# Attention with a running maximum: the pieces that find each row's maximum are computed for two heads at once, on half the rows of TensorE's array each

## The reference

```python
q = (x @ Wq).reshape(b, n, HEADS, DIM_HEAD).transpose(0, 2, 1, 3)
k = (context @ Wk).reshape(b, m, HEADS, DIM_HEAD).transpose(0, 2, 1, 3)
v = (context @ Wv).reshape(b, m, HEADS, DIM_HEAD).transpose(0, 2, 1, 3)
scores = jnp.einsum('bhnd,bhmd->bhnm', q, k) * scale
attn = jax.nn.softmax(scores, axis=-1)
out = jnp.einsum('bhnm,bhmd->bhnd', attn, v)
out = out.transpose(0, 2, 1, 3).reshape(b, n, HIDDEN)
return out @ Wo + bo
```

## Time and profile before

| | us |
|---|---|
| median of 3 runs | 1034.98 (1029.81 to 1036.09) |
| profiled execution | 1032.15 |
| its span, first to last instruction | 1030.3 |
| mean granted TensorE clock | 0.967 of full speed |
| busy: PE / weight loads / DVE / ACT / POOL | 947.4 / 556.1 / 586.7 / 360.5 / 563.2 |

### The profile page before, as it was taken

How to read it: one execution, slowest core, us unless ns; L and a number is a source line. 1 busy time by engine, 2 the same in 40 slices (tenths; PEclk the granted TensorE clock), 3 DMA queues, 4 the chain that set the end, 5 groups by cost and what they waited for, 6 DMA issues and landing times. The chain is left out here.

```text
span 1030.3 us, 12668 instructions
## 1 busy us (share of the span) xinstructions
PE 947.4 (92%) x3784; PEld 556.1 (54%) x3785; DVE 586.7 (57%) x1212; ACT 360.5 (35%) x506; POOL 563.2 (55%) x346
## 2 busy tenths in 40 slices
PE   6978699999999999999999999999899999999940
PEld 3544355555565555565555555545578888666620
DVE  5997566666667667657668658653744122144424
ACT  2254244434434434425443425443441111122202
POOL 4452187797767787767779768774005200022224
PEclk9998899999999999999999999999899999999975
DMA  8214600100001100001100001030593100322215
GB/s 272 57 41 122 168 11 11 32 0 11 11 1 52 31 1 11 11 0 51 31 11 0 11 8 45 11 106 38 171 342 141 41 1 0 122 78 84 75 36 168
DMA packets 45730, 62.19 MB, mean 60 GB/s; under 512 B 3600, under 2 KB 35216, under 8 KB 45680
## 3 DMA queue, kind: packets, MB, share of 16 engines
q1 hardware_dynamic: 40160, 53.85, 17.7%
q0 software_dynamic: 2256, 6.17, 1.7%
q10 hardware_dynamic: 3264, 1.57, 0.5%
HBM read 36.45 MB, written 17.59 MB: 52 GB/s over the span
## 5 line engine op out<-in xcount | busy, mean ns | idle before, releaser
L641 POOL TENSOR_TENSOR accG<-accG,probs 128x1024 f32<-128x1024 f32 (+1 forms) x170 | 404.1, 2377 | 59.9 <-ACT probs L675 44.9
L728 DVE TENSOR_REDUCE mxp<-mx 128x1 f32<-128x402 f32 x480 | 260.5, 571 | 97.4 <-PE mx L851 81.5
L675 ACT ACTIVATE probs<-st 128x1024 f32<-128x1024 f32 (+1 forms) x208 | 211.4, 1025 | 278.6 <-PE st L874 156.3
L886 PE MATMUL av<-probs,V 128*64 128x512 f32 (+1 forms) x832 | 192.4, 600 | 0.0
L874 PE MATMUL st<-Q,K 65*128 65x512 f32 (+1 forms) x416 | 159.1, 400 | 0.0
L886 PEld LDWEIGHTS av<-probs,V 128*64 128x64 f32 (+1 forms) x832 | 54.1, 136 | 102.4 <-issue 90.2
L851 PE MATMUL mx<-K,Q1b 128*128 128x400 f32 (+1 forms) x256 | 98.2, 384 | 1.2 <-DVE Q1b L716 0.9
L874 PEld LDWEIGHTS st<-Q,K 65*128 65x128 f32 (+1 forms) x416 | 75.7, 185 | 24.0 <-issue 12.4
L851 PE MATMUL mx<-K,Q1a 128*128 128x402 f32 x224 | 85.9, 383 | 0.2
L641 POOL TENSOR_TENSOR accG<-probs 128x1024 f32<-128x1024 f32 x16 | 38.2, 2386 | 79.9 <-ACT probs L675 68.1
L1512 POOL DMA_INDIRECT scratch_routed<-ysb,row x31 | 29.8, 961 | 85.1 <-DMA scratch_routed<-ysb,row 53.9
(11 more groups left out here) (196 smaller groups left out, 1184.4 us busy)
## 6 DMA issues: line engine op xcount, KB each, us to landing
w_gate_up<-in_gate_up SPq DMA_DIRECT2D x4, 2048.0 KB, 19.7
w_down<-in_down SPq DMA_DIRECT2D x2, 2048.0 KB, 14.8
xs<-scratch_sorted_x SPq DMA_DIRECT2D x31, 128.5 KB, 2.1
scratch_sorted_x<-zero SPq DMA_DIRECT2D x7, 514.0 KB, 7.6
K<-K SPq DMA_DIRECT2D x8, 400.5 KB, 4.8
xT<-in_xT SPq DMA_DIRECT2D x4, 512.0 KB, 8.5
xring<-in_x SPq DMA_DIRECT2D x4, 512.0 KB, 8.5
scratch_x1b<-xT SPq DMA_DIRECT2D x4, 512.0 KB, 3.3
```

The costliest lines, as they stand in the source:

```text
L641: pool.tensor_tensor(accG[0:r], so_far[0:r], probs[0:r, (p * KT + t) % RING], ALU.add).then_inc(g_add, 1)
L675: act.activation(probs[0:r, s], st[g % 2][0:r, :], ACT.Exp, scale=DH ** -0.5).then_inc(a_probs, 1)
L728: dve.tensor_reduce(mxp[:, par, u, j:j + 1], mx[(par + n) % 2][:, 0:kn], AX.X, ALU.max).then_inc(v_mx, 1)
L886: mm = pe.matmul(av[h * DH:(h + 1) * DH, :], V[0:r, t, (2 * p + h) * DH:(2 * p + h + 1) * DH], probs[0:r, g % RING, h * QC:(h + 1) * QC], ...
```

## The change

A piece now uses the high part of the queries alone, which is one half of the array's rows. The two heads' pieces for the same queries and keys are issued as a pair: head 0 on rows 0 to 63 into bank 0, head 1 on rows 64 to 127 into bank 1. For this the second head's queries are stored the other way round, low part on partitions 0 to 63 and high part on 64 to 127; the sum over all 128 rows is the same. A step has 16 pairs instead of 32 pieces. The first matmul of a pair waits for both reductions of the pair before, VectorE waits for both matmuls and then reduces twice. Every tile has one pair, behind `scores_2`; tiles 5, 9 and 11 have a second one between `scores_1` and `scores_2`. Nothing stands between the two matmuls of `scores_2` any more. The divisions come after pairs 5 and 10. SyncE copies the high part in two transfers.

```diff
 def query_high(_):
-        act.activation(Q1[0:DH, h], banks[2][DH * h:DH * h + DH, :], ACT.Copy).then_inc(a_q0, 1)
+        act.activation(Q1[DH * h:DH * h + DH, h], banks[2][DH * h:DH * h + DH, :], ACT.Copy).then_inc(a_q0, 1)
...
-PIECES_AT = (1, 1, 3, 3, 3, 3, 3, 3, 2, 3, 3, 2, 2)
-DIVIDE_AFTER = (11, 11, 22, 22)
+TWO_PAIRS_AT = (5, 9, 11)
+PIECE_PAIRS = QT * len(KC)
+DIVIDE_AFTER = (5, 5, 10, 10)
...
-                sp.dma_start(Q2[0:DH, par].bitcast(F32), Q1[par][0:DH].bitcast(F32)).then_inc(d_q2[par], 16)
+                for h in range(2):
+                    sp.dma_start(Q2[0:DH, par, h].bitcast(F32), Q1[par][DH * h:DH * h + DH, h].bitcast(F32)).then_inc(d_q2[par], 16)
...
-                act.activation(Q1[par][0:DH, h], mx[par][DH * h:DH * h + DH, :], ACT.Copy).then_inc(a_hi, 1)
+                act.activation(Q1[par][DH * h:DH * h + DH, h], mx[par][DH * h:DH * h + DH, :], ACT.Copy).then_inc(a_hi, 1)
...
             def piece_maxima(F, par, after_piece):
 
-                for u in range(2 * QT):
+                for i in range(QT):
                     for j, (k0, kn) in enumerate(KC):
-                        n = len(KC) * u + j + 1
-                        dve.wait_ge(p_mx, F * (STEP_MX - 1) + n)
-                        dve.tensor_reduce(mxp[:, par, u, j:j + 1], mx[(par + n) % 2][:, 0:kn], AX.X, ALU.max
-                                          ).then_inc(v_mx, 1)
+                        n = len(KC) * i + j + 1
+                        dve.wait_ge(p_mx, F * (STEP_MX - 1) + 2 * n)
+                        for h in range(2):
+                            dve.tensor_reduce(mxp[:, par, h * QT + i, j:j + 1], mx[h][:, 0:kn], AX.X, ALU.max
+                                              ).then_inc(v_mx, 1)
                         after_piece(n)
...
             def max_scores(F, pair, par, use, n, after=None):
 
-                u, j = (n - 1) // len(KC), (n - 1) % len(KC)
-                h, i = u // QT, u % QT
+                i, j = (n - 1) // len(KC), (n - 1) % len(KC)
...
-                pe.wait_ge(v_mx, use + (n - 1))
-                pe.matmul(mx[(par + n) % 2][:, 0:kn], Q1[par][:, h, i * P:(i + 1) * P], K1[:, 2 * pair + h, k0:k0 + kn],
-                          start=True, stop=True).then_inc(p_mx, 1)
+                pe.wait_ge(v_mx, use + (2 * n - 1))
+                for h in range(2):
+                    rows = slice(DH * h, DH * h + DH)
+                    pe.matmul(mx[h][:, 0:kn], Q1[par][rows, h, i * P:(i + 1) * P], K1[rows, 2 * pair + h, k0:k0 + kn],
+                              start=True, stop=True).then_inc(p_mx, 1)
...
                     for t in range(2, KT):
                         scores_1(c, p, t)
+                        if t in TWO_PAIRS_AT:
+                            next_piece()
+                        scores_2(c, p, t)
                         next_piece()
-                        scores_2(c, p, t, next_piece)
-                        if PIECES_AT[t] > 2:
-                            next_piece()
```

More of the change, by code:

```diff
@@ L354, in query_low @@
                     dve.wait_ge(a_q0, h + 1)
-                    dve.tensor_tensor(Q1[DH:P, h], banks[2][DH * h:DH * h + DH, :], Q1[0:DH, h].bitcast(F32), ALU.subtract
+                    dve.tensor_tensor(Q1[DH - DH * h:P - DH * h, h], banks[2][DH * h:DH * h + DH, :],
+                                      Q1[DH * h:DH * h + DH, h].bitcast(F32), ALU.subtract
                                       ).then_inc(v_q0, 1)
@@ L715, in q_low @@
                     dve.wait_ge(a_hi, F * 2 + (h + 1))
-                    ins = dve.tensor_tensor(Q1[par][DH:P, h], mx[par][DH * h:DH * h + DH, :],
-                                            Q1[par][0:DH, h].bitcast(F32), ALU.subtract).then_inc(v_lo, 1)
+                    dve.tensor_tensor(Q1[par][DH - DH * h:P - DH * h, h], mx[par][DH * h:DH * h + DH, :],
+                                      Q1[par][DH * h:DH * h + DH, h].bitcast(F32), ALU.subtract).then_inc(v_lo, 1)
                 dve.wait_ge(v_lo, F * 2 + 2)
@@ L798, in chunk @@
                     else:
-                        for n in range(1, STEP_MX):
+                        for n in range(1, PIECE_PAIRS + 1):
                             after_piece(n)
@@ L864, in scores_1, with scores_2 @@
                               start=True, stop=False)
-            def scores_2(c, p, t, between=None):
+            def scores_2(c, p, t):
                 g, r = p * KT + t, rows_of(t)
@@ L869, in scores_2 @@
                 if t == 0:
-                    pe.wait_ge(d_q2[par], (c * 2 + (p // 2 + 1)) * 16)
+                    pe.wait_ge(d_q2[par], (c * 2 + (p // 2 + 1)) * 32)
                     pe.wait_ge(d_m[par], (c * 2 + (p // 2 + 1)) * 32)
@@ L875, in scores_2 @@
                                    Q2[0:DH + 1, par, h], start=False, stop=True)
-                    if h == 0 and between is not None:
-                        between()
                 mm.then_inc(p_qk, 1)
@@ L945, in next_piece @@
                         done[0] += 1
-                        if ahead and done[0] < STEP_MX:
+                        if ahead and done[0] <= PIECE_PAIRS:
                             max_scores(F, pair, par, use, done[0], c * QT if p == 1 and not first else None)
```

## The result

The changed kernel takes 1145.1 us, the median of four runs (1127.5 to 1156.0), against 1033.6 for the kernel before (four runs, 1029.8 to 1036.1). The ratio is 1.096, 95% interval 1.086 to 1.106; it is taken without the two longest runs (1156.0 and 1153.5, mean granted clock 0.900), and the two others took 1136.7 and 1127.5 at 0.921 and 0.928. I had forecast slower, 1086 us with a range to 1126: the direction is right, half of the size is missing, and every run lies above the range. The profile shown is of the execution of 1156.0 us, so it shows the clock at its worst.

The account below looks back on a forecast made before the run. The prediction took a two-bank handshake between TensorE and VectorE as the bound, not a busy engine. Stages of 24.02 against 20.61 us give +3.41 a step, +51 over 15 steps: 1083 profiled, 1086 us median, range 1062 to 1126.

Parts of the forecast that it names:

- The handshake: Between successive pairs in the attention stages: a pair waits for both reductions of the one before, at least 1.61 us.
- the same four terms: From pair to pair: matmul to reduction 0.39 us, two reductions 1.06, release of the weight load 0.06, unhidden weight load 0.10.
- Stages 7.47, 7.47, 9.08: Forecast us for a step's three stretches with pairs, A, B and C, against 7.42, 6.84 and 6.35 before.
- the +51 us: Forecast growth over 15 attention steps, from +3.41 us a step in the three stages.
- Side by side: In each pair: its two half-row matmuls run at once, so a pair takes the time of one piece.
- The rival of a serial pair: A pair's two matmuls run one after the other: +6.3 us a step, 1126 to 1129 us; chance 12%.
- Switches: Changing array shape into half rows: 0.19 us into a first pair of each stage; on the way out inside the handshake.
- Cheap handshake: Rival for the stages: weight load hidden and no switch, +1.5 us a step, 1055 to 1058 us; chance 7%.
- PE relieved: Rival: stages bound by PE's columns, so halving helps: 3.6 us less a step, 978 to 981 us; chance 4%.
- the fourth rival: Clock: PE waits more, a third of the stages fall to 1.2 GHz, +66 us on top, about 1150; chance 4%.
- The sign that the prediction itself gave for being wrong: In the stages: a granted clock under 1; also listed were one-pair tiles under 1.5 us or stage C under 7.
- the price of a tile: In stages at 1.2 GHz: 0.92 us of score matmuls becomes 1.84 and the pair adds 0.2, 1.1 us a tile.

Follow-up runs that it names:

- more columns in the waits: Changed kernel with the two scores_1 matmuls of tiles 1, 5, 9 and 11 issued a second time while PE waits for the pair's reductions: 1092.6 us.
- short reductions: Every reduction reads 100 of 400 columns: 1038.8 us on the changed kernel (pairs), 1005.6 us on the kernel before (single pieces on full rows).
- pairs, own waits: Changed kernel, but each matmul of a pair waits only for its own bank and each reduction only for its own matmul: 1077.3 us.
- pairs, own waits and in the values: Changed kernel with separate bank waits for each matmul of a pair, and second pairs moved into the blocks of values: 1067.7 us.
- pairs, three in the values: Changed kernel with the second pairs of tiles 5, 9 and 11 moved into the three blocks of values, divisions after pairs 6 and 11: 1091.4 us.
- pairs on the same half: Changed kernel, but both matmuls of a pair take rows 0 to 63, so they run one after the other: 1261.8 us.

## Where the prediction was right, and where it failed

**The handshake.** Right. "From one pair to the next it takes at least 1.61 us": 1.63 measured, from the same four terms. Stages 7.47, 7.47, 9.08 were 7.55, 7.55, 9.18, and the +51 us were +55. The run with more columns in the waits, which keeps the clock behind the first step, is 63 us above the kernel before beside it (1092.6 against 1029.8): the 55, and some 6 us by which the lower clock lengthens its first step more than that of the kernel before.

**Side by side.** Right: the two records of a pair last 0.45 us together, as long as a single half-row piece (208.76 above), and on full rows, one after the other, the handshake is 0.15 longer. The rival of a serial pair falls.

**Switches.** Right in size: 0.2 us each way, shown by the half-row pieces in the order of before (0.39 for two). The Trainium skill, TensorEngine Tiling (Array Packing), Key Properties, says that a change of tiling mode drains the engine. 65 rows against 64, both matmuls in a row, agree with it here: stage B at full clock is 8.15 us with the one and 8.32 with the other. The weight of the switches was understated: short reductions show that the switches alone make pairs dearer than single pieces.

**Cheap handshake, PE relieved.** Both fall. The second would have needed the reductions out of the way, and with them nearly out of the way the pairs still lose by 33 us.

**Where it failed.** The step is the clock. The sum took it at 1.00 in all stages, a term put at nothing, and the fourth rival, which named its fall, got 4% with the reason that "no wait would exceed about 1 us". That reason was wrong: no wait of a pair's load was longer than 1.0 us, and the clock fell all the same, 0.89 over the steps behind the first, 69 of the 124 us in the profiled execution. The sign that the prediction itself gave for being wrong, a granted clock under 1 in the stages, came. The form was right (1.2 GHz in some of the stages), and so was the price of a tile (1.1 us forecast, 2.63 less 1.63 measured). That "about 1150" is close to the measured 1145 is in part luck: it charged four tiles a step and nothing to the blocks of values, which lost half. What was wrong is the chance, and that the range ended at 1126 although that case was named.

I had looked for one long wait. What the runs show instead is a combination. The waits in the table are those of weight loads and matmuls of pieces for reductions, summed over the profiled execution:

| run | rows of a piece | switches for pieces | PE waits for reductions, us | clock, whole run | clock, steps behind the first |
|---|---|---|---|---|---|
| kernel before | 128 | none | 62 | 0.967 | 1.00 |
| kernel before, 65 rows | 65 | none | 61 | 0.963 | 1.00 |
| pairs, full rows | 128 | none | 236 | 0.966 | 0.99 |
| pairs, 65 rows | 65 | none | 224 | 0.914 | 0.91 |
| pairs, short reductions | 64 | 32 a step | 28 | 0.958 | 1.00 |
| pairs, own waits | 64 | 32 a step | 62 | 0.960 | 0.99 |
| pairs, own waits and in the values | 64 | 32 a step | 75 | 0.945 | 0.97 |
| pairs, three in the values | 64 | 32 a step | 128 | 0.930 | 0.94 |
| the changed kernel | 64 | 32 a step | 162 | 0.900 | 0.89 |
| the same, more columns in the waits | 64 | 32 a step | 110 | 0.963 | 1.00 |
| pairs on the same half | 64 | 32 a step | 143 | 0.842 | 0.79 |
| single pieces on half rows | 64 | 64 a step | 110 | 0.775 | 0.70 |

Long waits with pieces on full rows hardly move the clock, nor do pieces on about half of the rows where the waits sum to no more than before, with 32 switches or without. Pieces on half of the rows together with longer waits, or with 64 switches, let it fall. Full-height matmuls in the waits give it back. Among the runs whose pairs run side by side the clock is the lower the longer the waits (28, 62, 75, 128, 162 us), save where more columns fill them. The order of the others is not explained by one number, and by what measure the chip decides is not shown.

The Trainium skill, TensorE: Matmul & The Clock Gate, A second HAM failure mode: psum-queue depth-cycling, tells of a kernel whose many short pauses between groups of matmuls made the clock swing. The falls of the changed kernel agree with it. The run on full rows, with more waiting and five short falls, shows that pauses alone did little here.

**What was not tried.** Whether a low part of zeros on full rows holds the clock as the real one does, and by how much each single pair brings the fall nearer. Why the fall hits only some of the steps, which are alike in order, is left open.

## What to carry to other kernels

Before two alternating buffers are filled at once, add up the chain from one filling to the next (start to consumer, both consumers, release, bare weight load) and compare it with what the producer has to do in between: here 1.63 us against two alternating 0.58s. A half-row matmul or pair among full-height ones pays 0.2 us on the way in and 0.2 on the way out, here more than the columns it saves; whether several pairs in a row would pay was not tried. And a change that leaves TensorE waiting, on part of its rows, is to be priced with the clock at its lower level over some stages, even when every wait is short.

## What the runs showed that I had not expected

- The clock of the changed kernel fell with no wait of a pair over 1.0 us. With the same order and both matmuls of a pair one after the other it depended on the rows in use: 0.966 on 128 rows, 0.914 on 65, 0.842 on 64 with switches.
- Extra work made the kernel faster: 8 more matmuls a step, at least 32 us less.
- At the lower clock pairs are 2.63 us apart, not 1.63. The weight loads at 544.22 and 546.85 wait for no reduction, so TensorE's own work sets this pace, and the block of values takes up to 6.2 us.
- Stages without pieces are not bound by TensorE (1.09 us a tile, 0.92 of matmuls), so a single piece adds less than its slot of 0.19: (5.96 - 4.36) / 11 = 0.15 us.
